# A graph network's first two projections moved tile by tile into the gather pass

## The reference, cut to what matters

```python
out_norm = clip(out_degree, 1) ** -0.5
in_norm = clip(in_degree, 1) ** -0.5
for i in range(3):
    h = h * out_norm[:, None]
    h = segment_sum(h[src], dst, num_segments=N)
    h = h * in_norm[:, None]
    h = h @ W[i] + b[i]
    if i < 2:
        h = relu(h)
```

## Time and profile before

| what | value |
|---|---|
| time, median of 3 runs | 8714.67 us (8711.82 to 8714.86) |
| profiled execution, first to last instruction | 6374.4 us |
| TensorE matmul / weight load busy | 76% / 40% of the span |
| VectorE, ScalarE, GpSimd busy | 62%, 33%, 66% |
| mean granted clock of TensorE | 0.717 of full speed |
| DMA, mean | 101 GB/s |

### The profile page before, as it was taken

One profiled execution on the slowest core, in us unless ns is written; L12 is line 12 of the kernel. 1 busy time (PEld: TensorE's weight loads), 2 busy tenths in 40 slices (PEclk: granted clock), 3 DMA queues, 4 the chain that ended last, 5 costly groups with the idle time before them and its releaser, 6 DMA issues.

```text
span 6374.4 us, 120359 instructions
## 1 busy us (share of the span) xinstructions
PE 4849.6 (76%) x15137; PEld 2567.8 (40%) x15138; DVE 3938.3 (62%) x12829; ACT 2134.1 (33%) x6879; POOL 4220.7 (66%) x4536
## 2 busy tenths in 40 slices
PE   2198898877877887899988766777777667777773
PEld 1133333343333334333333344445445445444441
DVE  7555555555555555455555565777777757777777
ACT  3100000020000002000000017888888368888883
POOL 2277777747777774777777406777776367777764
PEclk9956556576566668555555677888888778888886
DMA  1233333323333332333333313444443234444433
GB/s 56 66 105 105 105 105 105 105 90 106 106 106 106 106 106 88 108 105 105 105 105 105 114 56 106 110 111 110 110 110 93 64 104 110 110 111 110 106 97 121
DMA packets 353957, 645.83 MB, mean 101 GB/s; under 512 B 125955, under 2 KB 219841, under 8 KB 353442
## 3 DMA queue, kind: packets, MB, share of 16 engines
q0 software_dynamic: 200128, 549.85, 31.2%
q1 hardware_dynamic: 153346, 91.90, 5.1%
HBM read 592.75 MB, written 47.32 MB: 100 GB/s over the span
## 4 chain that ended last, share of the span: by engine, by line
PE 27%; issue 20%; POOL 17%; DVE 15%; DMA 13%; DVEq 5%; ACT 2%; POOLq 1%; SPq 1%; ACTq 0%
POOL ring L576 16%; PE main L821 12%; DMA ring<-conv_tab,idx 9%; PE main L947 7%; PE main L839 3%; DVE acc L1114 3%; DVE ring L1415 2%; DMA idx<-sidx 2%; DVEq L1114 2%; PE pso L866 2%; DVEq L1432 2%; DVE ring L1002 2%; PE psad L883 1%; POOL ring L615 1%; DVE ad L1309 1%
## 5 line engine op out<-in xcount | busy, mean ns | idle before, releaser
L821 PE MATMUL main<-ring,oh 128*128 128x257 f32 x4992 | 2684.5, 644 | 527.4 <-DMA ring<-conv_tab,idx 383.0
L576 POOL DMA_INDIRECT ring<-conv_tab,idx x2496 | 2366.2, 948 | 781.4 <-issue 610.9
L1114 DVE TENSOR_TENSOR acc<-acc,main 128x257 f32 (+1 forms) x4160 | 1767.7, 425 | 1356.4 <-PE main L821 969.8
L821 PEld LDWEIGHTS main<-ring,oh 128*128 128x128 f32 x4992 | 1156.1, 286 | 2054.7 <-DVE oh L1106 1405.5
L590 POOL DMA_INDIRECT ring<-attn_tab,idx x1664 | 1592.3, 957 | 542.3 <-issue 362.1
L947 PE MATMUL main<-ring,oh 128*128 128x264 f32 x3328 | 1262.1, 492 | 168.5 <-ACT ring L739 134.5
L1106 DVE TENSOR_SCALAR oh<-iota,dloc 128x128 f32<-128x128 f32 x2505 | 754.9, 302 | 453.7 <-PE main L821 281.1
L739 ACT ACTIVATE ring<-ring 128x64 f32<-128x64 f32 x3328 | 912.8, 340 | 47.9 <-issue 47.9
L653 ACT ACTIVATE nb<-acc 128x256 f32 (+1 forms) x147 | 58.6, 406 | 2235.3 <-DVE acc L1114 2108.4
L947 PEld LDWEIGHTS main<-ring,oh 128*128 128x128 f32 x3328 | 611.3, 226 | 348.9 <-ACT ring L739 220.3
L717 ACT ACTIVATE oh<-iota,dloc 128x128 f32<-128x128 f32 x1752 | 555.3, 391 | 20.2 <-DMA attn_tab<-oh 20.2
(11 more groups left out here) (202 smaller groups left out, 2796.7 us busy)
## 6 DMA issues: line engine op xcount, KB each, us to landing
ring<-conv_tab,idx POOLq DMA_INDIRECT x2496, 2.8
ring<-attn_tab,idx POOLq DMA_INDIRECT x1664
attn_tab<-oh SPq DMA_DIRECT2D x14, 910.0 KB, 4.3
conv_tab<-oh SPq DMA_DIRECT2D x14, 896.0 KB, 4.0
ring<-attn_tab SPq DMA_DIRECT2D x14, 896.0 KB, 4.8
sfl<-start_rows SPq DMA_DIRECT2D x424, 8.0 KB
efl<-end_rows SPq DMA_DIRECT2D x424, 8.0 KB
conv_tab<-acc SPq DMA_DIRECT2D x7, 896.0 KB, 14.5
```

The costliest lines, as they stand in the source:

```text
L576: pool.indirect_dma_start(ring3[:, j, 0:C], None, conv_tab[k], bass.IndirectOffsetOnAxis(ap=idx[:, (j // UH) * G + j % UH:(j // UH) * G + ...
L821: nc.tensor.matmul(main[j % 4][:, 0:C + 1], oh[:, (j % OHR) * P:(j % OHR + 1) * P], ring3[:, j, 0:C + 1], start=True, stop=True).then_inc( ...
L1114: nc.vector.tensor_tensor(a, a, main[k][:, 0:width], ALU.add).then_inc(added, 1)
```

## The change

In hops 0 and 1 there is a slot every 16 steps (`WIN`) of the gather pass, 52 (`NW`) in a hop, and 49 (`TAIL`) slots follow after it, 101 (`NS`) in all. In a slot one tile that is complete is copied, transposed, multiplied, scaled and stored, through the functions `feed_slot`, `turn_slot`, `copy_slot`, `multiply_slot`, `epilogue_slot`, `stage_slot` and `store_slot`. Which tile a slot takes stands in `slot_tile`, a table that VectorE works out before the first hop; a slot without a tile takes number 49, a spare accumulator and a spare piece of the table. Each slot stores 128 KB by a DMA of its own. The in-degree's root is worked out a tile at a time (`degree_slot`, `root_slot`).

Accumulators are not cleared in the hops: `merge` multiplies the accumulator by a column of `keep`, 0 where a tile begins and 1 elsewhere, and adds the product. The steps are laid out so that every tile but the last ends with the chunk that the next one begins with, even where a border falls on the border of a chunk. GpSimd waits before the next hop for the store of the last real tile. The ring's slots used in the hops are 64 instead of 32, and so are the steps in a loop's body; indices are fetched 16 at a time in four parts. The third hop has no slots and is projected after its pass, as before; the attention layers keep their order.

```diff
-U = 32
+U = 64
+WIN = 16
+NW = S // WIN
+TAIL = NT
+NS = NW + TAIL
...
+        def tables_done(k):
+
+            return SLOTS_OF + 16 * NS * k
...
+            def store_slot(k, w, j):
+
+                t = slot_index(sp.value_load(slot_tile[0:1, bass.ds(w, 1)], min_val=0, max_val=NT))
+                sp.wait_ge(slot_staged, w + (k * NS + 3))
+                sp.wait_ge(table_stored, w * 16 + tables_done(k))
+                sp.dma_start(conv_tab[k + 1].rearrange("(t p) c -> t p c", p=P)[bass.ds(t, 1), :, :]
+                             .rearrange("o p c -> (o p) c"), stage_of(j)).then_inc(table_stored, 16)
+
+            load_hop(0)
+            sp.wait_ge(steps_ready, 1)
+            for b in range(GB):
+                fetch_idx(b, b * G, G)
+            for k in range(HOPS):
                 if k < HOPS - 1:
-                    store_stage(conv_tab[k + 1], C, k, k + 1)
+                    with nc.sync.Fori(0, NW // GB - 1) as i:
+                        for b in range(GB):
+                            store_slot(k, i * GB + b, b)
+                            sp.wait_ge(products_done, CR + k * S + i * U + (b + 1) * G)
+                            fetch_idx(b, i * U + (GB + b) * G, G)
+                    for b in range(GB):
+                        store_slot(k, NW - GB + b, b)
+                        sp.wait_ge(products_done, CR + k * S + S - U + (b + 1) * G)
+                        fetch_idx(b, b * G, G)
+                    with nc.sync.Fori(0, TAIL // 2) as i:
+                        for b in range(2):
+                            store_slot(k, i * 2 + (NW + b), b)
+                    store_slot(k, NS - 1, NS - 1)
+                    sp.wait_ge(slot_proj, 2 + (k + 1) * NS)
+                    sp.wait_ge(slot_tmp, 2 + (k + 1) * NS)
+                    load_hop(k + 1)
...
-            def clear_first():
-                pool.wait_ge(table_stored, 16 * NI)
...
+            def gather_conv(k):
+                if k:
+                    last = pool.value_load(slot_tile[0:1, NS:NS + 1], min_val=1, max_val=NS)
+                    pool.wait_ge(table_stored, last * 16 + tables_done(k - 1))
                     pool.nop(nofuse=True)
...
+            def stage_slot(k, w, j):
+
+                t = tile_in(w)
+                act.wait_ge(slot_tmp, w + (k * NS + 3))
+                act.wait_ge(table_stored, w * 16 + (tables_done(k) - 16))
+                nc.scalar.activation(stage_of(j), tmp[:, (j % 2) * C:(j % 2 + 1) * C], ACT.Relu,
+                                     scale=onorm[:, bass.ds(t, 1)]).then_inc(slot_staged, 1)
...
+                if slots:
+                    turn_slot(k, NW, 0)
+                    with nc.tensor.Fori(0, TAIL // 2) as i:
+                        for b in range(2):
+                            turn_slot(k, i * 2 + (NW + b + 1), b + 1)
+                            multiply_slot(k, i * 2 + (NW + b), b)
+                    multiply_slot(k, NS - 1, NS - 1)
...
+            def merge(t, j, k, i):
+
+                dve.wait_ge(products_done, i * U + (CR + k * S + j + 1))
+                dve.wait_ge(added, i * U + (k * S + j + 4))
+                a = acc[:, bass.ds(t * AW, C + 1)]
+                nc.vector.scalar_tensor_tensor(out=a, in0=a, scalar=keep[:, bass.ds(i * U + j, 1)], in1=main[j % 4][:, 0:C + 1],
+                                               op0=ALU.mult, op1=ALU.add).then_inc(added, 1)
...
             def conv(k):
-                dve.wait_ge(table_stored, 16 * NI * (k + 1))
+                slots = k < HOPS - 1
+                dve.wait_ge(table_stored, tables_done(k))
                 if k:
                     dve.wait_ge(onehots, oh_base(k))
-                    dve.wait_ge(acc_clear, NT * (k + 1))
+                if slots:
+                    dve.wait_ge(w_in, 32 * (k + 1))
...
+                        if slots and k == 0 and j % WIN == 0:
+                            dve.wait_ge(added, i * U + (k * S + j + 4))
+                            degree_slot(w, b)
+                        if slots and j % WIN == 6:
+                            copy_slot(k, w, b)
+                        if slots and j % WIN == 10:
+                            epilogue_slot(k, w, b)
+                if not slots:
+                    return
+                dve.wait_ge(added, 4 + (k + 1) * S)
+                if k == 0:
+                    degree_slot(NW, 0)
+                copy_slot(k, NW, 0)
+                with nc.vector.Fori(0, TAIL // 2) as i:
+                    for b in range(2):
+                        if k == 0:
+                            degree_slot(i * 2 + (NW + b + 1), b + 1)
+                        copy_slot(k, i * 2 + (NW + b + 1), b + 1)
+                        epilogue_slot(k, i * 2 + (NW + b), b)
+                epilogue_slot(k, NS - 1, NS - 1)
```

More of the change, by code:

```diff
@@ L324, in gnn, with slot_index, stage_of @@
         HALF = 2 * P
+        SLOTS_OF = 16 * NI
+        SLOT_ROWS = 32 * P
         def oh_base(k):
             return k * (S + AHEAD)
+        def slot_index(value):
+            return nc.s_assert_within(value, 0, NT, skip_runtime_bounds_check_because="a tile, or the spare one, as the chip laid it out")
+        def stage_of(j):
+            return oh[:, SLOT_ROWS + (j % 2) * C:SLOT_ROWS + (j % 2 + 1) * C]
+        def tables_done(k):
+            return SLOTS_OF + 16 * NS * k
         QT = (NG + 2) * Q + 2
@@ L1212, in logit_columns @@
+            project(0, epilogue)
+            chain[0] += 4 * NT
+            row_scales(3, 2).then_inc(norm_ready, 1)
             def logit_columns(l):
```

380 lines of the change are left out of this document (233 added, 147 removed).

## The result

The changed kernel takes 9002.57 us (median, 8992.43 to 9006.93), the kernel before 8714.15 us on the same chip: a ratio of 1.0327, interval 1.0312 to 1.0341. It is 288 us slower. I had forecast 8679 us, 36 us faster.

What follows compares the result with a forecast made beforehand. POOL's gather issue was taken to bound the hops; the clear's -20.2, the first boundary's -0.3 and the second's -15.6 us summed to -36 us, a span of 6338 and a time of 8679 us, range 8611 to 8764.

Steps and rivals of the forecast that it cites:

- what lies around is left as it is: Whole run: the 2340.3 us between span 6374.4 and median 8714.67 stay constant; span differences carry over one to one.
- I leave 1.253 us: Inside a hop: POOL's gather spacing, 1.253 us, stays unchanged and hides the work added to VectorE and TensorE.
- an engine becomes the bound: Rival in the hops: a step costing 1.30 us outlasts POOL's spacing, +103 us, 8818; 0.09 together with something around the span.
- my 1.8: VectorE in the hops: copy, epilogue and two register loads of a slot add 1.8 us every 16 steps.
- The tail, L: Hop boundaries: period of a tail slot, 2.75 us in the first and 2.5 in the second; 2.15 to 2.8 given 0.45.
- My formula: POOL's stalls at the boundaries: 48 L - 43.6 in the first, 49 L - 50.2 in the second; 88.4 and 72.3 us.
- The clear: Before the first hop: 49 clearing copies go, so the first gather starts near 275.6 instead of 295.77, -20.2 us.
- gathers at 1.25 us in all hops: Sign in the hops: POOL keeps issuing gathers 1.25 us apart if the forecast holds.
- if POOL waits for products inside hop 0: Sign in hop 0: POOL waiting for products there would show the forecast wrong.
- 64 gathers, then a stop: Sign after each hop's end: POOL issues 64 gathers ahead, then stops.
- its end follows the 49th tail store by about 30 us: Sign at the boundaries: POOL's stop ends about 30 us after the 49th tail store.
- If the time around the span moves: Sign for the whole run: a change in the time taken to lie outside the span would show the forecast wrong.

## Why the prediction was wrong, step by step

**The step that failed first: "I work in differences of the span and carry them one to one to the median; what lies around is left as it is."** Nothing lies around: where before takes 8702.29 us its span is 8700.5. The 2340.3 us were time inside the stages, 1530 us in the hops, where VectorE's slow queue sets the pace, and 736 in the attention, which was not taken apart; the profile shown could not have it. I had the two numbers side by side, a span of 6374.4 and a time of 8714.67, and took the gap for a constant. It said that the profile was of a machine with another bound.

**Inside a hop, "I leave 1.253 us".** This term of the sum was mis-placed altogether: before is at 1.853 us a step on the long chip (1540.2/831), after at 2.011 in hop 0, for +130.6 us. I had named "an engine becomes the bound" as a rival, with VectorE's step as the quantity, gave a time for 1.30 us a step, and priced it at 0.09 together with everything around the span. That rival came true in kind, VectorE's queue being the bound, but it was the bound already before, and not through the data work that the rival added up. On the short chip the term holds as forecast: hop 0 took 1040.7 us, and VectorE's added work is hidden behind POOL.

What the slots themselves cost on a long chip can be read between hop 1, which has them, and hop 2, which has none, both after a tail of 5. Their lengths differ by 1636.3 - 1554.1 = 82.2 us, but hop 2 begins with a run of 80 gathers and hop 1 with one of 64. Past the first 96 gathers of each hop that unevenness is out, and the steps of the same run are 2.071 us in hop 0, 2.023 in hop 1 and 1.918 in hop 2; before has 1.874, 1.920 and 1.872 (hops 0 and 2 with 3 packets of code, hop 1 with 127). So body, loads of code and the multiply in place of the plain add make 0.046 us a step, the slots 0.105, which is 1.68 us for each, near my 1.8, and what hop 0 has beside them, probably the degrees, 0.048. These are differences between stretches of two runs on one chip, and no run takes one of the three out. Slots are not hidden on a long chip, as VectorE's queue is the bound there. The stop at a loop's end that I spread over 64 steps, 4.4 us, I had read in hop 1, where the code is loaded anew; in hop 0 of the same profile it is 0.95 us.

**The tail, L.** The mechanism was right: all 49 slots run, POOL stops after 64 gathers, and the stop ends a fixed time after the last store, 22 us in the first tail and 19 in the second, on both kinds of chip. But L is no single number. On the short chip L was 2.44 and 2.29 us where I took 2.75 and 2.5, and the stalls were 13.70 - 1.25 + 57.4 - 1.25 = 68.6 and 59.1 us instead of 88.4 and 72.3. My formula with the measured L gives 48 x 2.44 - 43.6 = 73.5 and 49 x 2.29 - 50.2 = 62.0. So form and constants were right within 5 us, and L was too high by 0.31 and 0.21 us; the second constant counts 16 us for the 16 steps that the first counts as 17. Beside POOL's gathers the second tail's slots take 2.46 us, as I had assumed, and after them 1.87, which I had not reckoned with. The sum by the Trainium skill ("DMA: Bandwidth & Descriptors", "Anatomy of one DMA"), about 2.0 us fixed and the bytes, fitted on GpSimd's path, gave an estimated L of 2.65 us. The trace does not agree for these stores of SP's: each waits for the one before, and once POOL stands still they follow each other every 1.87 us, 0.34 us of issue and the address included. On the long chip L was 3.84 in the first tail, above my upper bound of 3.5. And the ring worked against me: the first tail store came 10.9 us after the last gather on the short chip, as forecast (11.7), but 72 us after it on the long one, where up to 64 gathered steps were still to be added. Boundaries and stops together grew by 80 and 51 us.

**The clear.** Right: 273.81 us to the first gather, forecast 275.6; -21.2 us against -20.2.

```profile
273.81 0.95 POOL L641 DMA_INDIRECT ring<-conv_tab,idx  x1 [16.42 <-DMA idx<-sidx]
```

The table of slots was hidden, as I had said: the first gather waited for its indices alone, and VectorE's first multiply and add starts at 278.2 us.

**Of the signs I had named**, "gathers at 1.25 us in all hops" failed at once, and "if POOL waits for products inside hop 0" came true: 658.5 us of such waits in hop 0, as the group of the gathers in that window has it, against 37.8 us in hop 0 of the profile that I had read. But the kernel before has 377.8 us of them on a long chip too, and 168.9 for indices. "64 gathers, then a stop" and "its end follows the 49th tail store by about 30 us" held on both kinds of chip in kind; on the short one the last store was issued at 1443.01 and POOL resumed at 1464.81, 22 us later. "If the time around the span moves" could not happen, as there was none.

**Where the short chip's gain comes from.** The changed kernel's span is 6239.0 us there, 135.4 us under the 6374.4 of the profile shown before; the medians on one chip, 6242.07 and 6366.57, are 124.5 us apart, where the sum had 36. Of the 135.4 the way to the first gather is 21.5, the boundaries are 176.6 - 127.7 = 48.9 where I had 16, and 63.2 us lie in the attention and the end (2302.1 and 149.9 us against 2338.7 and 176.5). These two are not edited, but lie behind the larger ring and body. The body of 64 with its indices by 16 gave 23 to 40 us by itself, in the same place; why is open.

**What stays open.** Which thing makes the register instructions slow while POOL issues gathers in a row, and why only on some chips. It isn't the data path of VectorE or GpSimd, whose data instructions keep their durations, and it isn't the loading of code, of which hop 0 of the kernel before has next to none. It is tied to runs of gathers: it starts within them, ends soon after they end, and shorter runs took 6.8% off the kernel before. That is shown; the resource in common is not, and neither is whether POOL's own work or the transfers that it starts disturb the queues. Open is also how the 0.046 us a step that the changed kernel has without slots divide into the body, its loads of code and the multiply.

## What to carry to other kernels

Compare the profiled span with the timed runs before anything else: if they differ by more than a few us, the profile is not of what is timed, and its bound may not be the bound. An engine that issues transfers need not run as far ahead as its buffers allow; a lead of 8 on 32 slots cost nothing where the queues were quick and gave 6.8% where they were not, but a lead of 4 cost 1.5%. Empty iterations that each wait out a store are paid in full once they lie ahead of the next stage: 44 of them at each of two boundaries cost 185 us on a long chip. And a price is read in the stage where it will be paid: the stop at a loop's end was 4.4 us in hop 1 and 0.95 in hop 0.

## What the runs showed of the hardware that I had not expected

The same program takes 6367 to 6370 us on some chips and 8696 to 8714 on others, 37% apart, with equal durations of VectorE's and GpSimd's data instructions (add 424 ns, multiply and add 483 ns, gather 946 to 949 ns). The difference is in the queues. The register instruction of the changed kernel that works out the count of products to wait for (L1255, in `merge`), long chip and short chip:

```profile
L1255 DVEq ALU_OP  x2496: 1/45/729, 274.4 to 5536.2; - x192
```

```profile
L1255 DVEq ALU_OP  x2496: 40/45/47, 274.9 to 3532.8; - x192
```

And it isn't VectorE's alone. GpSimd's own are touched, up to 1396 ns; TensorE's are not in the hops, at most 36 ns, but in the attention up to 1271 ns (L945, against 36 on the short chip). SP's register work for the address of a slot's store, on the long chip:

```profile
L451 SPq MOVE conv_tab<-oh x202: 13/29/727, 339.1 to 3999.0; - x101
```
